# Dealing the pass into the last layer of a four-layer graph network to four engines

## The chip, the cores and the metric

The kernel runs on one core of one Trainium2 chip. The metric is the device time of one execution in microseconds (us); less is better. The profile is one such execution, recorded with every instruction of each engine: PE is TensorE, DVE is VectorE, ACT is ScalarE, POOL is GpSimd, SP is SyncE, and a name with a q (ACTq, SPq) is that engine's sequencer, where DMAs are issued.

## The reference

Four graph layers, each with a layer norm and a relu in front and a residual behind, over 100000 nodes with 64 features and 50000 edges:

```python
edge_index = jnp.stack([src, dst])
h = jnp.maximum(_layernorm(x, axis=-1), 0.0)
x = x + _L0_gnn_ref(h, edge_index, W3, b3, W4, b4)     # two SGConv layers
h = jnp.maximum(_layernorm(x, axis=-1), 0.0)
x = x + _L1_gnn_ref(h, edge_index, edge_attr_64, W, b, eps)
h = jnp.maximum(_layernorm(x, axis=-1), 0.0)
x = x + _L2_gnn_ref(h, attn_w, temp, src, dst)         # K = 8 steps of edge attention
h = jnp.maximum(_layernorm(x, axis=-1), 0.0)
x = x + _L3_gnn_ref(h, src, dst)                       # K = 10 steps
```

The last layer, `_L3_gnn_ref`, takes h = relu(layernorm(x)) as its features `feat`. It starts with `out = w[0] * feat` and adds `w[step + 1] * h` after each of ten steps of gather, scale, sum by destination and scale. So between the third and the fourth layer, every row of x is normed; the normed row is stored for the gathers, and w[0] times that row is added to x.

## The kernel before

Destinations that edges reach are "seats": 128 partitions by 392 columns, one row of 64 f32 each, resident in SBUF as `X`. The columns are worked in NCH = 28 chunks of CH = 14 columns (128 x 896 f32, 448 KB). The pass into the last layer, called pass e here, lies between the end of the attention steps and the first gather of the last layer. It runs over the 28 chunks, and each chunk c uses slot s = c % 2 of two row buffers, `row_be = [rowsB, rowsE]`. `rowsE` is a part of `wide_block`, by which name the profile calls it.

VectorE, for each chunk (`rows_of_e`): `spread_of` makes the variance of each of the 14 rows (14 bn_stats at L1570 and five small operations, L1573 to L1579) and raises `var_ready`. Then `add_rows` of the chunk two before (L2536) adds mix[0] times the made rows to X. Then `scales_of` (L2020, L2025) waits for ScalarE's square root, makes a scale and an offset for each row and raises `scales_ready`.

ScalarE (`seat_pass`): `root(CH)` is the square root (L958) of the next chunk's variance. `scaled_rows` makes the rows of this chunk, one ACTIVATE Relu with scale and bias for each of the 14 columns (L1112). It then waits for the last of them and issues the store of the chunk (L1116) to the table `tab` in HBM. The order is root(c + 1), then rows(c), and before rows(c) it waits on `seats_stored["e"][s]`, the store of the chunk two before.

GpSimd and TensorE have nothing to do in this pass. SyncE issues ten loads of "dead rows" (L547) as soon as the attention steps are over. When the pass is over, VectorE copies the gather indices (L2557), stages the two front rows, and GpSimd scatters the front row (`front_rows`, L575) and starts the gathers of the last layer (L571). X is read and written by the same engine, VectorE, with ScalarE reading it in between.

`Reached` is a register that counts the value awaited. FIRST is 1, a start value of the counting semaphores. `fresh()` clears VectorE's own step semaphore, by which it orders its dependent instructions (`nth()`).

`seat_pass` serves pass a too, the same pass into the first layer, with `row_ac` as its buffers. The functions that the change touches:

Of the kernel before, what the change touches and what calls it, by code (L numbers as in the profile page):

```python
# [3 lines left out]
def _build(nc, x, src, dst, edge_attr, W3, b3, W4, b4, W1, b1, eps, attn_w, temp, out):  # L4
# [7 lines left out]
    ALU = mybir.AluOpType  # L12
# [5 lines left out]
    N, E, D = _N, _E, _D  # L18
    HID = W3.shape[0]
    CH = 14  # L20
    NCH = 28
# [26 lines left out]
    with ctx:  # L48
# [3 lines left out]
        def sem(name):  # L52
            return ctx.enter_context(nc.semaphore(name))
# [21 lines left out]
        X = sb("X", [P, XC, D])  # L75
# [59 lines left out]
        mixb = sb("mixb", [P, K3 + 1])  # L135
        wk = sb("wk", [P, 1])
        scales = sb("scales", [P, 2, 2, CH])
# [3 lines left out]
        G = sb("G", [P, 2, CH, AW])  # L141
# [14 lines left out]
        xm = sb("xm", [P, CH, D])  # L156
        st = sb("st", [P, CH, 6])
        lnw = sb("lnw", [P, 6, CH])
# [107 lines left out]
        widest_loaded = sem("widest_loaded")  # L266
        order_ready = sem("order_ready")
        x_gathered = [sem("x_gathered0"), sem("x_gathered1")]
        x_front = sem("x_front")
        gathered = [sem("gathered0"), sem("gathered1")]  # L270
        gathered3 = [sem("gathered3_0"), sem("gathered3_1")]
# [70 lines left out]
        FIRST = 1  # L342
# [11 lines left out]
        def seat_rows(k, c):  # L354

            return seats(tab, SEAT0 + KINDS.index(k) % 2 * EP, c)
# [10 lines left out]
        def wide(t, n=D):  # L367

            return t.unsqueeze(2).to_broadcast([t.shape[0], t.shape[1], n])
# [25 lines left out]
        def staged_rows(k, c):  # L395

            at = KINDS.index(k) * D
            return staged[:, ds(c * CH, CH), at:at + D]
# [7 lines left out]
        def _(sp):  # L406
# [138 lines left out]
            sp.wait_ge(step_done, K2 + 1)  # L545
            for n in range(K3):
                sp.dma_start(dead_rows[n], staged_rows("e", n)).then_inc(dead_gathered, 16)  # L547
            for n in range(K3):
                sp.wait_ge(dead_ready, n + 1)
                sp.dma_start(seats(alt_e, 0, SPLIT + (n - 1) % K3), dead_rows[(n - 1) % K3]).then_inc(dead_stored, 16)  # L550

        @block.gpsimd
        def _(pool):
# [324 lines left out]
            def attention_end(to):  # L878

                front_sums(to, F_SEAT, F_TSEAT, AW)  # L880
                front_rows(to, F_SEAT_W, FR[:, 0, :], False)
                pool.wait_ge(step_done, r_sd.more(1))
                pool.sem_inc(pool_waited, 1)
# [6 lines left out]
                    attention_end(to)  # L890
            narrow_sweep(alt_d, K2, AW, gathered, gathered_rest)
            attention_end(even_d)
            for s in (0, 1):
                pool.wait_ge(seats_stored["e"][s], FIRST + 16 * NCH // 2)
            pool.sem_inc(pool_waited, 1)
            front_rows(tab, F_TAB_W, rowsE[:, 0, :])
# [51 lines left out]
        def _(act):  # L948
# [153 lines left out]
            def seat_pass(k, rows):  # L1102

                r_to = [Reached(act, f"act_pass_{k}{s}", FIRST) for s in (0, 1)]

                def scaled_rows(c, s):
                    act.wait_ge(seats_stored[k][s], r_to[s].reg)
                    r_to[s].skip(16)
                    act.wait_ge(scales_ready, r_scales.more(1))
                    part = X[:, ds(c * CH, CH), :]  # L1110
                    for j in range(CH):
                        last = nc.scalar.activation(rows[s][:, j, :], part[:, j, :], ACT.Relu,  # L1112
                                                    bias=scales[:, s, 1, j:j + 1], scale=scales[:, s, 0, j:j + 1])
                    last.then_inc(scaled, 1)
                    act.wait_ge(scaled, r_scaled.more(1))
                    act.dma_start(seat_rows(k, c), rows[s][:, :, :]).then_inc(seats_stored[k][s], 16)  # L1116

                root(CH)
                with act.Fori(0, NCH // 2 - 1) as i:
                    for s in (0, 1):  # L1120
                        root(CH)
                        scaled_rows(2 * i + s, s)
                root(CH)
                scaled_rows(NCH - 2, 0)
                scaled_rows(NCH - 1, 1)
                root(2)
# [260 lines left out]
        def _(dve):  # L1387
# [22 lines left out]
            def nth():  # L1410

                steps[0] += 1
                return steps[0]

            def fresh():

                dve.sem_clear(dve_step)
                steps[0] = 0
# [175 lines left out]
            def xcols(c):  # L1594
                return X[:, ds(c * CH, CH), :]
# [933 lines left out]
            with dve.Fori(2, K2 + 1) as k:  # L2529
                fresh()  # L2530
                step_d(k)
            def add_rows(c, s):

                dve.wait_ge(scaled, r_scaled.more(1))
                part = xcols(c)
                v.scalar_tensor_tensor(part, row_be[s][:, :, :], mixb[:, 0:1], part, ALU.mult, ALU.add).then_inc(dve_step, 1)  # L2536
                dve.wait_ge(dve_step, nth())

            def rows_of_e(c, s, before=None):

                spread_of(xcols(c), CH)
                if before is not None:
                    add_rows(before, s)
                scales_of(c, s)

            fresh()
            for s in (0, 1):
                rows_of_e(s, s)
            with dve.Fori(1, NCH // 2) as i:
                fresh()  # L2550
                for s in (0, 1):
                    rows_of_e(2 * i + s, s, 2 * i + (s - 2))
            for s in (0, 1):
                add_rows(NCH - 2 + s, s)
            for s in (0, 1):
                dve.wait_ge(seats_stored["e"][s], FIRST + 16 * NCH // 2)
            v.tensor_copy(idxC[:, :], idxA[:, :]).then_inc(dve_step, 1)  # L2557
# [167 lines left out]
```

## Time and profile before

| what | value |
|---|---|
| median of 3 runs | 8325.15 us (8324.16 to 8325.87) |
| the profiled execution, its time | 8323.41 us |
| its span in the trace | 8321.7 us |
| DVE busy | 5424.0 us (65%) |
| POOL busy | 5607.8 us (67%) |
| ACT busy | 822.4 us (10%) |
| PE busy | 1660.0 us (20%) |

Busy times are of the whole span of the program, whose stages have different limits; pass e is one short stage of it. The chain that ended last is the profile's own path from the last instruction back to the first: at each step to what released it, or to the instruction before it on its engine.

### The profile page before, as it was taken

What the parts mean: (1) busy time and instruction counts of PE and PEld (TensorE: products, weight loads), DVE (VectorE), ACT (ScalarE), POOL (GpSimd) and SP (SyncE); (2) the same over time, 40 slices, a digit from 0 to 9 for tenths busy, and PEclk for the clock granted to TensorE, in tenths of its full rate; (3) what the DMA queues carried; (4) which work ended last, traced back from release to release, by engine and by line L of the source; (5) the groups of instructions that cost most, each with busy time, mean ns of one, the idle gap of its engine ahead of it and who ended that gap; (6) DMA issues with size and microseconds to landing.
All of it is one profiled execution on the core that took longest, in us unless ns stands there. A gap on an engine that the chain in (4) does not pass through costs nothing.

```text
span 8321.7 us, 61168 instructions
## 1 busy us (share of the span) xinstructions
PE 1660.0 (20%) x7784; PEld 1203.9 (14%) x7784; DVE 5424.0 (65%) x18625; ACT 822.4 (10%) x2010; POOL 5607.8 (67%) x5356
## 2 busy tenths in 40 slices
PE   5744444211354035500022102000000000000000
PEld 1233333211243023400022101000000000000000
DVE  6778787768988633367788788666556664445520
ACT  0011111100121521100000000000006000000000
POOL 6777767647777767577677572666640767777777
PEclk8755555555555555555555555555555555555555
DMA  7033434210355334834444213143322222433310
GB/s 262 1 89 94 96 87 98 63 34 21 95 123 128 102 91 121 272 89 111 122 110 109 63 49 83 45 44 46 41 33 88 49 60 49 42 44 43 38 22 19
DMA packets 1198008, 661.32 MB, mean 79 GB/s; under 512 B 1057323, under 2 KB 1070560, under 8 KB 1195204
## 3 DMA queue, kind: packets, MB, share of 16 engines
q10 hardware_dynamic: 880608, 373.78, 16.3%
q0 software_dynamic: 174720, 155.54, 12.9%
q1 hardware_dynamic: 142436, 129.95, 5.3%
q14 instruction: 238, 1.95, 0.1%
q8 instruction: 6, 0.10, 0.0%
HBM read 236.69 MB, written 425.58 MB: 80 GB/s over the span
## 4 chain that ended last, share of the span: by engine, by line
DVE 37%; POOL 30%; issue 19%; DMA 6%; ACT 3%; PE 2%; DVEq 1%; ACTq 1%; POOLq 0%; SPq 0%
POOL G L571 18%; POOL X L571 7%; DVE G L2106 6%; DVE st L1570 4%; POOL out L575 4%; ACT wide_block L1112 2%; DVE xm L1587 2%; DVE X L1545 2%; DVE wide_block L1591 2%; PE TR L1271 1%; DVE X L1544 1%; POOL wide_block L571 1%; DVE G L2418 1%; DVE agg L1668 1%; DVE xm L1600 1%
## 5 line engine op out<-in xcount | busy, mean ns | idle before, releaser
L571 POOL DMA_INDIRECT G<-tab,idxA x1008 | 1079.4, 1071 | 344.5 <-issue 323.6
L571 POOL DMA_INDIRECT X<-flagtab,X x588 | 624.5, 1062 | 231.1 <-issue 230.2
L571 POOL DMA_INDIRECT G<-alt_e,idxC x420 | 435.8, 1038 | 145.9 <-issue 133.4
L575 POOL DMA_INDIRECT seatmap<-X x392 | 406.4, 1037 | 165.2 <-issue 129.0
L571 POOL DMA_INDIRECT X<-lookup,X x392 | 424.5, 1083 | 132.9 <-issue 126.3
L571 POOL DMA_INDIRECT X<-in_x,dst_gat x392 | 423.7, 1081 | 124.9 <-issue 124.9
L1261 PE MATMUL TR<-w4T,shared 128*128 128x64 f32 x2356 | 468.8, 390 | 156.5 <-ACT shared L976 156.5
L571 POOL DMA_INDIRECT G<-alt_d,idxC x392 | 399.3, 1019 | 142.2 <-issue 135.5
L1570 DVE BATCH_NORM_STATS2 st<-xin 128x6 f32<-128x64 f32 x3136 | 419.3, 211 | 114.6 <-issue 62.2
L1261 PEld LDWEIGHTS TR<-w4T,shared 128*128 128x128 f32 x2356 | 455.4, 300 | 250.1 <-issue 250.1
L1278 PE MATMUL HP<-ident,tcar 128*64 128x128 f32 (+1 forms) x21 | 8.7, 415 | 2263.2 <-DVEq L1495 2252.6
L1238 PE MATMUL TR<-ident,wide_block 128*128 128x128 f32 x882 | 219.0, 425 | 773.8 <-DVEq L1637 534.1
L958 ACT ACTIVATE lnw<-lnw,lneps 128x14 f32<-128x14 f32 (+1 forms) x340 | 104.3, 307 | 2633.6 <-DVEq L1581 2581.0
L2585 DVE TENSOR_TENSOR G<-G,chn 128x320 f32<-128x320 f32 (+2 forms) x165 | 82.7, 534 | 407.7 <-DMA G<-alt_e,idxC 202.6
L571 POOL DMA_INDIRECT shared<-in_edge_attr,eidx x252 | 284.2, 1128 | 79.4 <-issue 79.1
L2106 DVE SCALAR_TENSOR_TENSOR G<-G,chn 128x64 f32<-128x64 f32 x1092 | 312.1, 286 | 39.1
L1278 PEld LDWEIGHTS HP<-ident,tcar 128*64 128x64 f32 (+1 forms) x21 | 3.2, 150 | 2266.5 <-issue 2266.5
L1271 PE MATMUL TR<-w1Te,hT 64*128 64x64 f32 x1568 | 182.0, 420 | 731.3 <-ACT hT L966 731.3
L571 POOL DMA_INDIRECT G<-even_e,idxC x252 | 261.6, 1038 | 83.4 <-issue 74.0
L571 POOL DMA_INDIRECT G<-tab,idxC x252 | 260.0, 1032 | 79.7 <-issue 79.7
L575 POOL DMA_INDIRECT out<-X,dst_out x252 | 244.9, 972 | 97.5 <-issue 81.8
L966 ACT ACTIVATE hT<-TR 128x512 f32<-128x512 f32 (+1 forms) x358 | 183.9, 537 | 1209.6 <-PE TR L1238 1190.3
(517 smaller groups left out, 7671.0 us busy)
## 6 DMA issues: line engine op xcount, KB each, us to landing
tab<-wide_block ACTq DMA_DIRECT2D x294, 448.0 KB, 3.8
tab<-rowsB ACTq DMA_DIRECT2D x98, 448.0 KB, 2.7
xin<-tab SPq DMA_DIRECT2D x84, 448.0 KB
raw<-G ACTq DMA_DIRECT2D x84, 448.0 KB
xin<-in_x SPq DMA_DIRECT2D x56, 448.0 KB
tab<-wide_block ACTq DMA_DIRECT2D x2, 12544.0 KB, 56.3
out<-shared ACTq DMA_DIRECT2D x56, 448.0 KB, 5.8
staged<-wide_block SPq DMA_DIRECT2D x20, 1120.0 KB, 5.9
```

The source lines that it names most:

```text
L571: pool.indirect_dma_start(to, None, table, bass.IndirectOffsetOnAxis(ap=index, axis=0), bounds_check=bound, oob_is_err=False).then_inc(s, 16)
L575: pool.indirect_dma_start(table, bass.IndirectOffsetOnAxis(ap=index, axis=0), frm, None, bounds_check=bound, oob_is_err=False).then_inc(s, 16)
L966: last = nc.scalar.activation(hT[:, a:b, :].rearrange("p a b -> p (a b)"), T[:, a * P:b * P], ACT.Copy)
L1112: last = nc.scalar.activation(rows[s][:, j, :], part[:, j, :], ACT.Relu, bias=scales[:, s, 1, j:j + 1], scale=scales[:, s, 0, j:j + 1])
L1238: last = nc.tensor.transpose(T[:, q * P:(q + 1) * P], rows[:, 2 * q:2 * q + 2, :].rearrange("p a b -> p (a b)"), ident[:, :])
L1261: last = nc.tensor.matmul(T[:, r * D:(r + 1) * D], U[:, r % 2, r // 2, :], w4T[:, :], start=True, stop=True)
L1271: last = nc.tensor.matmul(T[:, at:at + D], hT[h * D:(h + 1) * D, r // 2, :], w[h * D:(h + 1) * D, :], start=True, stop=True)
L1545: v.tensor_scalar(hot_lo[:, j % NHOT, :], iota16[:, :], chn[:, 1, j:j + 1], None, ALU.is_equal).then_inc(dve_step, 1)
L1570: last = v.bn_stats(st[:, r, :], xr[:, r, :])
L1587: v.scalar_tensor_tensor(xm[:, a0:a1, :], wide(m_sum[:, a0:a1]), -0.5, xr[:, a0:a1, :], ALU.mult, ALU.add)
L1591: v.scalar_tensor_tensor(to, xm[:, 0:R, :], 0.0, wide(rs), ALU.max, ALU.mult).then_inc(dve_step, 1)
L2106: v.scalar_tensor_tensor(G[:, s, j, 0:W], before, go[:, j:j + 1], G[:, s, j, 0:W], ALU.mult, ALU.add).then_inc(dve_step, 1)
```

## The change

In pass e, the work on a chunk is dealt out anew. Pass a stays as it was.

- ScalarE makes the first 11 (`SHARE = CH - 3`) of the 14 rows and no longer waits for its own last row to issue the store. It also waits on `added[s]`, the addition of the chunk two before, since X and the row buffers are shared with GpSimd.
- VectorE makes the other three rows by two operations on 128 x 192 (subtract the mean into `xm`, then relu and scale into `row_be`), after `scales_of` of the chunk. Ahead of the second it waits for the store and the addition of the chunk two before. Its loop over pairs is written out as 28 chunks, and `add_rows` is gone from it.
- GpSimd, idle until now, waits for both parts of the chunk, multiplies all 14 rows by mix[0] into `G`, and adds `G` to X.
- SyncE waits for both parts of the chunk and issues the store. In its queue this stands behind the ten loads of the dead rows.

```diff
@@ semaphores
+        added = [sem("added0"), sem("added1")]
+        last_rows = sem("last_rows")
+        SHARE = CH - 3
@@ SyncE, behind the ten loads of dead rows
+            for c in range(NCH):
+                sp.wait_ge(scaled, NCH + c + 1)
+                sp.wait_ge(last_rows, c + 1)
+                sp.dma_start(seat_rows("e", c), row_be[c % 2][:, :, :]).then_inc(seats_stored["e"][c % 2], 16)
@@ GpSimd, behind attention_end
+            for c in range(NCH):
+                s = c % 2
+                part = X[:, c * CH:c * CH + CH, :]
+                pool.wait_ge(scaled, NCH + c + 1)
+                pool.wait_ge(last_rows, c + 1)
+                pool.tensor_scalar(G[:, s, :, 0:D], row_be[s][:, :, :], mixb[:, 0:1], None, ALU.mult).then_inc(pool_step, 1)
+                pool.wait_ge(pool_step, r_step.more(1))
+                pool.sem_inc(pool_waited, 1)
+                pool.tensor_tensor(part, part, G[:, s, :, 0:D], ALU.add).then_inc(added[s], 1)
             for s in (0, 1):
+                pool.wait_ge(added[s], FIRST + NCH // 2)
                 pool.wait_ge(seats_stored["e"][s], FIRST + 16 * NCH // 2)
@@ ScalarE, scaled_rows
                     act.wait_ge(scales_ready, r_scales.more(1))
+                    if k == "e":
+                        act.wait_ge(added[s], r_added[s].reg)
+                        r_added[s].skip(1)
                     part = X[:, ds(c * CH, CH), :]
-                    for j in range(CH):
+                    for j in range(CH if k == "a" else SHARE):
...
                     last.then_inc(scaled, 1)
-                    act.wait_ge(scaled, r_scaled.more(1))
-                    act.dma_start(seat_rows(k, c), rows[s][:, :, :]).then_inc(seats_stored[k][s], 16)
+                    if k == "a":
+                        act.wait_ge(scaled, r_scaled.more(1))
+                        act.dma_start(seat_rows(k, c), rows[s][:, :, :]).then_inc(seats_stored[k][s], 16)
@@ VectorE
-            def add_rows(c, s):
-
-                dve.wait_ge(scaled, r_scaled.more(1))
-                part = xcols(c)
-                v.scalar_tensor_tensor(part, row_be[s][:, :, :], mixb[:, 0:1], part, ALU.mult, ALU.add).then_inc(dve_step, 1)
-                dve.wait_ge(dve_step, nth())
-
-            def rows_of_e(c, s, before=None):
+            def rows_of_e(c, s):
 
                 spread_of(xcols(c), CH)
-                if before is not None:
-                    add_rows(before, s)
                 scales_of(c, s)
-
-            fresh()
+                part = X[:, c * CH + SHARE:c * CH + CH, :]
+                v.scalar_tensor_tensor(xm[:, SHARE:CH, :], wide(lnw[:, 0, SHARE:CH]), -0.5, part,
+                                       ALU.mult, ALU.add).then_inc(dve_step, 1)
+                dve.wait_ge(dve_step, nth())
+                if c >= 2:
+                    dve.wait_ge(seats_stored["e"][s], FIRST + 16 * (c // 2))
+                    dve.wait_ge(added[s], FIRST + c // 2)
+                v.scalar_tensor_tensor(row_be[s][:, SHARE:CH, :], xm[:, SHARE:CH, :], 0.0,
+                                       wide(scales[:, s, 0, SHARE:CH]), ALU.max, ALU.mult).then_inc(dve_step, 1)
+                dve.wait_ge(dve_step, nth())
+                dve.sem_inc(last_rows, 1)
+
             for s in (0, 1):
-                rows_of_e(s, s)
-            with dve.Fori(1, NCH // 2) as i:
-                fresh()
-                for s in (0, 1):
-                    rows_of_e(2 * i + s, s, 2 * i + (s - 2))
+                dve.sem_inc(added[s], FIRST)
+            for c in range(NCH):
+                if c % 2 == 0:
+                    fresh()
+                rows_of_e(c, c % 2)
             for s in (0, 1):
-                add_rows(NCH - 2 + s, s)
+                dve.wait_ge(added[s], FIRST + NCH // 2)
```

## Rows read from the trace of the kernel before

**Rows 1.** Timeline of ScalarE, start of pass e: start us, us, engine, line, operation.

```profile
6267.14 0.31 ACT L958 ACTIVATE lnw<-lnw,lneps 128x14 f32<-128x14 f32 x1 [11.19 <-DVEq L1581]
6270.85 0.31 ACT L958 ACTIVATE lnw<-lnw,lneps 128x14 f32<-128x14 f32 x1 [3.41 <-DVEq L1581]
6271.07 4.74 ACT L1112 ACTIVATE rowsB<-X,scales 128x64 f32 x14
6275.98 0.34 ACTq L1116 DMA_DIRECT2D tab<-rowsB  x1
6276.43 0.31 ACT L958 ACTIVATE lnw<-lnw,lneps 128x14 f32<-128x14 f32 x1 [0.62 <-ACT rowsB L1112]
6276.67 4.74 ACT L1112 ACTIVATE wide_block<-X,scales 128x64 f32 x14
6281.57 0.34 ACTq L1116 DMA_DIRECT2D tab<-wide_block  x1
6282.25 0.31 ACT L958 ACTIVATE lnw<-lnw,lneps 128x14 f32<-128x14 f32 x1 [0.84 <-ACT wide_block L1112]
```

**Rows 2.** Busy time of each engine in the stretch of pass e.

```profile
6264.35:6431.71 167.36, 0.00 (x0) 0.00 (x0) 116.49 (x617) 139.28 (x420) 0.00 (x0) 0.50 0.32 98
```

**Rows 3.** Timeline of VectorE, the first two chunks of pass e.

```profile
6264.35 1.87 DVE L1570 BATCH_NORM_STATS2 st<-X 128x6 f32<-128x64 f32 x14 [0.37 <-DVE eidx L2331]
6266.26 0.18 DVE L1573 TENSOR_TENSOR lnw<-st 128x14 f32<-128x14 f32 x1
...
6266.87 0.17 DVE L1579 SCALAR_TENSOR_TENSOR lnw<-lnw 128x14 f32<-128x14 f32 x1
6267.47 0.24 DVE L2020 RECIPROCAL scales<-lnw 128x14 f32<-128x14 f32 x1 [0.43 <-ACT lnw L958]
6267.75 0.17 DVE L2025 SCALAR_TENSOR_TENSOR scales<-lnw,scales 128x14 f32<-128x14 f32 x1
6268.07 1.87 DVE L1570 BATCH_NORM_STATS2 st<-X 128x6 f32<-128x64 f32 x14
...
6276.00 1.15 DVE L2536 SCALAR_TENSOR_TENSOR X<-rowsB,mixb,X 128x896 f32 x1 [1.16 <-ACT rowsB L1112]
```

**Rows 4.** Timeline of all engines, end of pass e.

```profile
6424.32 4.74 ACT L1112 ACTIVATE wide_block<-X,scales 128x64 f32<-128x64 f32 x14 [0.50 <-ACT rowsB L1112]
6429.10 0.35 ACTq L1116 DMA_DIRECT2D tab<-wide_block  x1
6431.71 0.36 DVE L2557 COPY idxC<-idxA 128x392 int32<-128x392 int32 x1 [1.46 <-DMA tab<-wide_block]
```

**Rows 5.** Groups of VectorE by line and shape: busy us, mean ns of one.

```profile
L1587 DVE SCALAR_TENSOR_TENSOR xm<-lnw,X 128x320 f32<-128x320 f32 x112 | 50.1, 489 | 8.8 <-DVE lnw L1579 8.8
L1587 DVE SCALAR_TENSOR_TENSOR xm<-lnw,X 128x256 f32<-128x256 f32 x56 | 23.7, 423 | 0.0
```

**Rows 6.** Groups of GpSimd by line and shape, computing operations.

```profile
L615 POOL COPY X<-X 125x800 f32<-125x800 f32 x1 | 1.0, 1034 | 6.0 <-DMA X<-seatmap 6.0
L587 POOL IOTA X<- 128x800 f16 x1 | 0.8, 802 | 0.2 <-POOL X L584 0.2
L591 POOL MEMSET ident<- 128x128 f32 x1 | 0.2, 204 | 0.2 <-POOL X L587 0.2
```

**Rows 7.** Timelines of GpSimd and of VectorE around GpSimd's copy.

```profile
585.16 1.03 POOL L615 COPY X<-X 125x800 f32<-125x800 f32 x1 [5.98 <-DMA X<-seatmap]
...
584.32 1.09 DVE L1591 SCALAR_TENSOR_TENSOR wide_block<-xm,lnw 128x896 f32<-128x896 f32 x1
```

**Rows 8.** Timeline of all engines, in the last layer.

```profile
6460.99 4.25 DVE L2096 SCALAR_TENSOR_TENSOR G<-G,chn 128x64 f32<-128x64 f32 x13
6461.07 1.00 POOL L571 DMA_INDIRECT G<-tab,idxC  x1 [0.30 <-issue]
6462.37 1.01 POOL L571 DMA_INDIRECT G<-tab,idxC  x1 [0.30 <-issue]
```

**Rows 9.** DMA issues of pass e's stretch: count, size, us to landing.

```profile
tab<-rowsB ACTq DMA_DIRECT2D x14, 448.0 KB, 2.5
xin<-staged SPq DMA_DIRECT2D x2, 448.0 KB, 7.3
```

**Rows 10.** Timeline of SyncE's queue, its last issues in pass e.

```profile
6273.48 4.16 SPq L547 DMA_DIRECT2D wide_block<-staged  x2
```

More of the change, by code:

```diff
@@ L1104, in seat_pass @@
                 r_to = [Reached(act, f"act_pass_{k}{s}", FIRST) for s in (0, 1)]
+                r_added = [Reached(act, f"act_added_{k}{s}", FIRST) for s in (0, 1)]
                 def scaled_rows(c, s):
@@ L2531, in _ @@
                 step_d(k)
-            def add_rows(c, s):
-                dve.wait_ge(scaled, r_scaled.more(1))
-                part = xcols(c)
-                v.scalar_tensor_tensor(part, row_be[s][:, :, :], mixb[:, 0:1], part, ALU.mult, ALU.add).then_inc(dve_step, 1)
-                dve.wait_ge(dve_step, nth())
-            def rows_of_e(c, s, before=None):
-                spread_of(xcols(c), CH)
-                if before is not None:
-                    add_rows(before, s)
-                scales_of(c, s)
-            fresh()
-            for s in (0, 1):
-                rows_of_e(s, s)
-            with dve.Fori(1, NCH // 2) as i:
-                fresh()
-                for s in (0, 1):
-                    rows_of_e(2 * i + s, s, 2 * i + (s - 2))
+            def rows_of_e(c, s):
+                spread_of(xcols(c), CH)
+                scales_of(c, s)
+                part = X[:, c * CH + SHARE:c * CH + CH, :]
+                v.scalar_tensor_tensor(xm[:, SHARE:CH, :], wide(lnw[:, 0, SHARE:CH]), -0.5, part,
+                                       ALU.mult, ALU.add).then_inc(dve_step, 1)
+                dve.wait_ge(dve_step, nth())
+                if c >= 2:
[5 more added lines that the diff above has]
+                dve.sem_inc(last_rows, 1)
+            for s in (0, 1):
+                dve.sem_inc(added[s], FIRST)
[3 more added lines that the diff above has]
+                rows_of_e(c, c % 2)
             for s in (0, 1):
-                add_rows(NCH - 2 + s, s)
+                dve.wait_ge(added[s], FIRST + NCH // 2)
             for s in (0, 1):
```

## The prediction

> **What bounds the kernel now.** I read the page first. VectorE and GpSimd are busy for about two thirds of the span and ScalarE for a tenth, but these are averages over stages. The change touches one stage only, the pass into the last layer, so I went to the windows view for that stretch. From the first bn_stats at 6264.35 to the copy of the indices at 6431.71 it takes 167.4 us, 2.0% of the span. ScalarE is busy for 139.3 us of it, VectorE for 116.5, GpSimd for nothing [rows 2]. Then the timeline of ScalarE: 14 rows take 4.74 us. Around them stand the wait for the last row, the issue of the store (0.34), the root and the loop's branch. From the root at 6270.85 to the root at 6282.25 two chunks lie, 11.4 us, so 5.70 a chunk, in which the engine only waits for itself [rows 1]. VectorE is not late: its addition starts when the rows are there [rows 3]. So ScalarE bounds the pass. Outside of the chunks there is a start (the first rows begin at 6271.07, 6.72 us in) and an end: the last row is made at 6429.06, and the pass ends 2.65 us later, when the last store has landed [rows 1, 4].
>
> **ScalarE's part.** Fourteen rows take 4.74, the last of them about 0.42 whole, so one every 0.332 us and eleven take 3.74. The root costs 0.22 (6270.85 to 6271.07) [rows 1]. The wait for the last row and the issue (0.6 to 0.8 us of idle time ahead of the root) go, and one wait that is as a rule satisfied comes. ScalarE alone would need some 4.1 to 4.3 us a chunk. This would be a gain of 1.5 us a chunk, 40 us in all, if nothing else became late.
>
> **VectorE's part.** The addition (1.15 us) goes. The spread takes 6264.35 to 6267.04, 2.69; the root's round trip 0.43; reciprocal and offset up to the next bn_stats 0.60 [rows 3]. Two new operations of 192 elements come. The same form takes 0.489 us at 320 and 0.423 at 256, so 0.36 at 192 [rows 5]; with the 0.15 us that each of its dependent steps waits (6267.92 to 6268.07 [rows 3]) both are 1.02. Sum 4.74 us a chunk. That the loop is written out takes its branch away, which lay in VectorE's spare time: nothing.
>
> **GpSimd's part.** The trace of before shows it multiplying or adding nowhere. The nearest rows are a copy of 800 elements, 1.03 us, and an iota of 800, which only writes, 0.80 [rows 6]. For the product (one input, 896 elements) this gives 0.90 by the iota and 1.16 by the copy; I take 1.0. The sum has two inputs. At least the second input costs what the first adds to the iota, 1.03 + 0.23 = 1.26 at 800 or 1.41 at 896; at most it costs a second copy, 2.3. I take the middle, 1.85. Between the two stands 0.17, as between its steps at the start (0.2 idle [rows 6]). Together P = 3.0 us, from 2.5 to 3.6. The Trainium skill (GPSIMD Engine Reference, section 3.1) measured 4497 ns for an add of 2048 f32. Scaled to 896 this is an estimate of 1.97 us; with it the sum below would come out 3 us later. No run here shows it yet.
>
> **SyncE's part.** The store's issue leaves ScalarE. It is queued behind ten loads of dead rows, whose issue ends at 6277.6 [rows 10] and which take 7 us to land [rows 9]. The first chunk is ready at about 6275.8, so the first store is some us late, once: 0 to 3 us. Later stores land 2.5 us after their issue [rows 9], 2.8 with the wait ahead, a little less than P, so they are hidden behind GpSimd.
>
> **The wait that comes.** VectorE writes its three rows into the slot of the chunk two before. So it waits for that chunk's addition, and behind it in its queue stand the spread of the next chunk, with it ScalarE's next root, and with it ScalarE's rows. The ring over two chunks is: addition seen 0.2, three rows 0.36 + 0.15, spread 2.69, root 0.10 + 0.22, eleven rows 3.74, seen by GpSimd 0.2, then P. That is 7.66 + P = 10.7, or 5.33 a chunk, if each engine ran at its own pace. The great saving on ScalarE shrinks to 0.37 a chunk before any collision.
>
> **The collision.** The copy of GpSimd began at 585.16, while VectorE's operation with two SBUF inputs ran until 585.41. It took 1.03, which is 0.23 more than the iota of the same length, and 0.25 us of it lay beside that operation [rows 6, 7]. It can be read as a copy that waited for VectorE to let go of SBUF. Against it speaks that GpSimd's indirect DMAs take their usual 1.00 us right beside thirteen such operations, and these their usual time too [rows 8]; but an indirect DMA is no stream over the tile. The Trainium skill (SBUF — State Buffer, "Who interferes with whom") says that a VectorE instruction with two SBUF inputs and a GpSimd instruction that reads SBUF exclude each other for a whole instruction, and that it is the later one that blocks. By that rule the sum is the one below; without it, the ring's. The copy's row agrees, weakly.
>
> What it costs here if they exclude each other: eight of VectorE's operations of a chunk have two SBUF inputs, all but bn_stats and the reciprocal. After a spread, ScalarE's rows end 0.32 + 3.74 later, and GpSimd starts at 4.26. VectorE starts the next bn_stats 0.43 + 0.60 + 1.02 = 2.05 after the same point, ends them at 3.93 and is between 3.96 and 4.74 in its five small operations, just when GpSimd comes. They need SBUF by turns: VectorE stands for the product, slips one small operation in, and stands for the sum. A chunk is then 4.74 + 1.0 + 1.85 = 7.59 us.
>
> **The sum.** Start: 6.72, the 1.02 of chunk 0's own three rows, eleven rows 3.74: 11.5. Then 26 chunks by 7.59: 197.3. The last chunk has no spread behind it: 3.9. The end: 0.2, P, 0.2: 3.4. Together 216.1, against 167.4: 48.7 us more. The profiled execution took 8323.41 and the median of the runs is 8325.15; on the median this is 8374. By the other reading it is 11.5 + 26 by 5.33 + 3.9 + 3.4 = 157.4, 10 us less. The two are even at 5.72 us a chunk, and 0.2% (16.7 us, about what a measurement of this kernel can tell from no change) slower begins at 6.36.
>
> **The rivals.**
> 1. They exclude each other (the forecast): 7.59 a chunk, 8374. With P's parts from 2.31 to 3.46 it is 7.05 to 8.20, so 8359 to 8390. Chance 0.55.
> 2. They exclude each other for one of the two operations only, because the small ones of VectorE are through before the product begins, or because the product doesn't hold them: 4.74 + 1.0 to 4.74 + 1.85, thus 5.7 to 6.6 a chunk, 8326 to 8348. Chance 0.08.
> 3. No exclusion, the ring bounds: 5.33 a chunk, 8315; with P from 2.5 to 3.6 and up to 3 us for the late first store 8309 to 8327. For it speak the indirect DMAs of rows 8. Chance 0.27.
> 4. GpSimd is much dearer than its copy, with no exclusion. The ring passes 5.72 a chunk when P is over 3.8, and 6.36 when P is over 5.1; at P = 6, 6.8 a chunk, 8357. Nothing but the lack of a row speaks for it. Chance 0.06.
> 5. The other side: the buffers don't bind and VectorE's own 4.74 a chunk does: 11.5 + 123.2 + 7.3 = 142, 25 us less, 8300. For that P would have to be under 1.8 and the store to land within 1.6 us, and neither row allows it [rows 6, 9]. Chance 0.04.
>
> The range that holds the time 8 times in 10 goes from 8312, in the middle of rival 3, to 8394, a bit above rival 1's end. The likeliest case's own is 8359 to 8390. Faster by over 0.2%: rival 5 and the edge of rival 3, 0.06. Slower by over 0.2%: rival 1, the upper halves of rivals 2 and 4, 0.63. Within: 0.31.
>
> **What the changed profile would show.** ScalarE: groups of eleven rows in 3.74 us, no store. GpSimd: 28 products and 28 sums; their starts, one from the next, give P. VectorE: if there is exclusion, one of L1573 to L1579 stands for an us or more beside GpSimd's product or sum, in its own duration or as a gap ahead of it, in nearly every chunk, and chunks come every 7 to 8 us. If not, the small operations keep their 0.1 us steps beside GpSimd, and the only long wait of VectorE is ahead of its second new operation, on the addition of two chunks before, with chunks every 5.3 us. What follows the pass shouldn't change. The forecast is wrong if GpSimd's reads go on beside VectorE's, or if they take turns by element and not by instruction.

## The result and the profile after

Over 14 runs each, the changed kernel takes 8338.13 us (8334.27 to 8346.81) and the kernel before 8324.65 us (8316.77 to 8331.14). The ratio is 1.0018 with an interval of 1.0011 to 1.0025: a little slower, just inside the 0.2% that I took as no change. The forecast was 8374, 49 us more; 13.5 us more came. The measured time lies in the range, but the range reached from the middle of rival 3 to beyond rival 1 and so says little; the forecast move is over three times too large.

The profiled execution took 8338.17 us. Its pass e runs from the first bn_stats at 6262.47 to the copy of the indices at 6447.8, so 185.3 us against 167.4 [rows 2], 17.9 us more. The whole execution is 14.8 us longer; the other 3 us lie outside the pass, less than the executions scatter there.

First, the windows view of that stretch. Its columns are, here and in [rows 2], the length in us, the busy us (and number of instructions) of PE, PE's weight loads, DVE, ACT and POOL, the clock granted to TensorE, the share of the DMA engines, and GB/s:

```profile
6262.47:6447.80 185.33, 0.00 (x0) 0.00 (x0) 141.97 (x645) 112.50 (x336) 124.78 (x56) 0.50 0.29 89
```

ScalarE's work fell from 139.3 to 112.5 us. VectorE's rose from 116.5 to 142.0, though its additions of 1.15 us each are gone. GpSimd has 124.8. No engine is busy for the whole stretch, so a chain over engines sets the pace. The groups of GpSimd in the pass:

```profile
L908 POOL TENSOR_TENSOR X<-X,G 128x896 f32<-128x896 f32 x28 | 54.0, 1928 | 5.1 <-POOL G L905 5.1
L905 POOL TENSOR_SCALAR G<-wide_block,mixb 128x896 f32<-128x896 f32 x14 | 35.4, 2530 | 18.9 <-ACT wide_block L1133 18.9
```

And the two groups of VectorE, in the stretch 6264 to 6430, that take much longer than their work:

```profile
L2559 DVE SCALAR_TENSOR_TENSOR xm<-lnw,X 128x192 f32<-128x192 f32 x27 | 26.6, 985 | 4.0
L2047 DVE SCALAR_TENSOR_TENSOR scales<-lnw,scales 128x14 f32<-128x14 f32 x27 | 22.4, 831 | 0.9
```

The sum takes 1.93 us, as I had it (1.85). The product takes 2.53 us, and I had 1.0. VectorE's offset, 0.17 us when alone, takes 0.83 on average, and the mean's subtraction 0.99 in place of 0.36. The reason shows in the timeline of the first meeting, GpSimd's product of chunk 0 beside VectorE's spread of chunk 2:

```profile
6274.10 2.53 POOL L905 TENSOR_SCALAR G<-rowsB,mixb 128x896 f32<-128x896 f32 x1 [17.48 <-ACT rowsB L1133]
6274.18 0.95 DVE L1599 TENSOR_TENSOR lnw<-lnw 128x14 f32<-128x14 f32 x1
6275.16 0.17 DVE L1601 SCALAR_TENSOR_TENSOR lnw<-lnw 128x14 f32<-128x14 f32 x1
...
6276.82 1.95 POOL L908 TENSOR_TENSOR X<-X,G 128x896 f32<-128x896 f32 x1 [0.19 <-POOL G L905]
```

L1599 starts inside the product and takes 0.95 us in place of 0.17. It ends 1.03 us after the product's start, while the product goes on for 1.5 us more, beside the next operation, which keeps its 0.17. So the product keeps VectorE out for about its first microsecond only. From the middle of the pass, where the pace has settled:

```profile
6341.54 1.94 POOL L908 TENSOR_TENSOR X<-X,G 128x896 f32<-128x896 f32 x1 [0.18 <-POOL G L905]
6341.67 1.84 DVE L2047 SCALAR_TENSOR_TENSOR scales<-lnw,scales 128x14 f32<-128x14 f32 x1
6343.66 0.36 DVE L2559 SCALAR_TENSOR_TENSOR xm<-lnw,X 128x192 f32<-128x192 f32 x1
6344.06 0.36 DVE L2565 SCALAR_TENSOR_TENSOR rowsB<-xm,scales 128x192 f32<-128x192 f32 x1
6344.57 1.87 DVE L1592 BATCH_NORM_STATS2 st<-X 128x6 f32<-128x64 f32 x14 [0.15 <-DVE rowsB L2565]
...
6345.18 2.53 POOL L905 TENSOR_SCALAR G<-wide_block,mixb 128x896 f32<-128x896 f32 x1 [1.70 <-ACT wide_block L1133]
6346.47 0.18 DVE L1595 TENSOR_TENSOR lnw<-st 128x14 f32<-128x14 f32 x1
...
6347.09 0.17 DVE L1601 SCALAR_TENSOR_TENSOR lnw<-lnw 128x14 f32<-128x14 f32 x1
6347.35 0.31 ACT L975 ACTIVATE lnw<-lnw,lneps 128x14 f32<-128x14 f32 x1 [2.27 <-DVEq L1603]
6347.62 3.75 ACT L1133 ACTIVATE rowsB<-X,scales 128x64 f32 x11
...
6351.47 2.53 POOL L905 TENSOR_SCALAR G<-rowsB,mixb 128x896 f32<-128x896 f32 x1 [1.68 <-ACT rowsB L1133]
```

Here the ring can be followed. The sum of one even chunk ends at 6343.48. VectorE's offset L2047 began 0.13 us after that sum and ended with it, so the sum keeps it out to its end. But VectorE needs that very sum for its rows two operations later, so nearly all that it stands for would have been a wait anyway. Its rows are done at 6344.42, the next spread at 6347.26, the root starts at 6347.35, ScalarE's rows end at 6351.37 and GpSimd begins at 6351.47. Product, 0.18 and sum end at 6356.12: 12.64 us for two chunks, 6.32 each. Later in the pass the sum meets the operation behind L2047, the mean's subtraction:

```profile
6398.01 1.90 POOL L908 TENSOR_TENSOR X<-X,G 128x896 f32<-128x896 f32 x1 [0.18 <-POOL G L905]
6398.26 1.87 DVE L2559 SCALAR_TENSOR_TENSOR xm<-lnw,X 128x192 f32<-128x192 f32 x1
```

There less work is left behind the sum, and the products come every 6.18 us. Over chunks 2 to 26 they start 6.23 us apart on average.

### The profile page after: what moved, and what is told of

It is laid out like the page before. It is cut to its first block and busy times, and to the rows that moved or that the text cites. A ratio compares the mean times of both kernels' runs of the same rounds, so it can differ in the third digit from the quotient of the medians.

```text
span 8336.5 us, 60751 instructions
## 1 busy us (share of the span) xinstructions
PE 1684.4 (20%) x7784; PEld 1223.0 (15%) x7784; DVE 5448.3 (65%) x18653; ACT 795.5 (10%) x1926; POOL 5731.8 (69%) x5412
## 5 line engine op out<-in xcount | busy, mean ns | idle before, releaser
L1609 DVE SCALAR_TENSOR_TENSOR xm<-lnw,xin 128x320 f32<-128x320 f32 (+1 forms) x672 | 279.1, 470 | 34.0 <-DVE lnw L1601 25.8
```

The source lines that it names most:

```text
L1609: v.scalar_tensor_tensor(xm[:, a0:a1, :], wide(m_sum[:, a0:a1]), -0.5, xr[:, a0:a1, :], ALU.mult, ALU.add)
```

## The experiments

All compare pass e, from the first bn_stats to the copy of the indices, in the profiled execution; the time of the whole kernel scatters by some us even where nothing is changed, so of kernels with one run only the pass is judged. "Ring" is the reading that the chain over two chunks sets the pace; "exclusion" is that of my forecast, that VectorE's work plus the time it stands shut out of SBUF sets it. P is GpSimd's part of a chunk, product, gap and sum, 4.64 us in the changed kernel.

| kernel | pass, us | a chunk, us | median time, us | ratio to before |
|---|---|---|---|---|
| before | 167.4 | 5.70 | 8324.65 | |
| changed | 185.3 | 6.18 to 6.32 | 8338.13 | 1.0018 [1.0011, 1.0025] |
| 1, no multiply and add | 151.8 | 5.0 | 8312.22 (one run) | |
| 2, product contiguous | 188.5 | | 8346.17 (one run) | |
| 3, immediate scalar | 185.6 | | 8334.80 (one run) | |
| 4, next spread first | 178.1 | 6.07 | 8344.37 | 1.0013 [1.0004, 1.0022] |
| 5, SyncE's stores alone | 158.1 | 5.31 | 8322.75 | 0.9987 [0.9978, 0.9996] |
| 6, 14 rows on ScalarE | 168.7 | 5.64 | 8330.10 | 0.9996 [0.9987, 1.0005] |
| 7, product as tensor_tensor | 205.6 | 7.15 | 8380.21 (one run) | |
| 8, one input from PSUM | 186.7 | 6.30 | 8344.78 (one run) | |
| 9, seven and eight | 174.6 | 5.85 | 8340.47 (one run) | |
| 10, four and eight | 149.9 | 4.88 | 8310.76 | 0.9974 [0.9965, 0.9984] |
| 11, five, written out | 148.5 | 4.87 | 8311.79 | 0.9975 [0.9965, 0.9985] |

The pace of a chunk is half the distance of every other root or product in the middle of the pass. The kernel before, measured again beside the experiments, had 8329.60 us (one run) beside 1 to 3, 8333.62 beside 4 to 7 and 8331.35 beside 8 to 11. The changed kernel's ratio is to 8324.65, the others' are to these, so times of different groups are not compared with each other.

**1. GpSimd waits and signals, but computes nothing.** The addition to X is left out.

```diff
-                pool.tensor_scalar(G[:, s, :, 0:D], row_be[s][:, :, :], mixb[:, 0:1], None, ALU.mult).then_inc(pool_step, 1)
-                pool.wait_ge(pool_step, r_step.more(1))
-                pool.sem_inc(pool_waited, 1)
-                pool.tensor_tensor(part, part, G[:, s, :, 0:D], ALU.add).then_inc(added[s], 1)
+                pool.sem_inc(added[s], 1)
```

> GpSimd waits and signals as in the changed kernel, but multiplies and adds nothing: the addition of mix[0] times the rows to X is left out. In the changed kernel the pass takes 185.4 us, 6.3 a chunk. Ring theory (the ring over two chunks sets the pace, and VectorE's standing beside GpSimd costs at most 0.4 us a chunk): the ring is now closed by the store, which lands 2.8 us after the rows, so (0.1 + 0.36 + 0.15 + 2.69 + 0.10 + 0.27 + 3.75 + 2.8) / 2 = 5.1 us a chunk and a pass of about 151 us. Exclusion theory (VectorE's chunk plus what it stands for SBUF): nothing to stand for, so VectorE's own 4.74 a chunk, a pass of about 142 us. Both: L1599, L2047 and L2559 of VectorE are back at 0.17, 0.17 and 0.36 us in every chunk.

The pass took 151.8 us, as the ring has it, and the stretched operations are back at their own lengths. VectorE's busy time in the pass is 104.1 us where the changed kernel has 142.0, with 644 and 645 instructions. So in the changed kernel VectorE stands shut out for 37.8 us in all, 1.35 a chunk.

```profile
6265.87:6417.72 151.85, 0.00 (x0) 0.00 (x0) 104.14 (x644) 112.47 (x336) 0.00 (x0) 0.50 0.35 109
```

VectorE now waits a little for the store, ahead of its rows:

```profile
6348.72 0.36 DVE L2556 SCALAR_TENSOR_TENSOR xm<-lnw,X 128x192 f32<-128x192 f32 x1
6349.58 0.36 DVE L2562 SCALAR_TENSOR_TENSOR wide_block<-xm,scales 128x192 f32<-128x192 f32 x1 [0.51 <-DMA tab<-wide_block]
```

So GpSimd's two operations are worth 33.5 us of the pass, and the slot's ring is closed by the next thing, the store, when they are gone.

**2 and 3. Why the product is dear.** Two suspects: the pitch of its output (the rows of G lie 67 elements apart, with 64 in use), and its scalar, which it reads from SBUF by a pointer. In experiment 2 the sum reads the product from the contiguous buffers too (not shown):

```diff
-                pool.tensor_scalar(G[:, s, :, 0:D], row_be[s][:, :, :], mixb[:, 0:1], None, ALU.mult).then_inc(pool_step, 1)
+                pool.tensor_scalar([rowsA, hT as 14 x 64][s], row_be[s][:, :, :], mixb[:, 0:1], None, ALU.mult).then_inc(pool_step, 1)
+++ in the other kernel
+                pool.tensor_scalar(G[:, s, :, 0:D], row_be[s][:, :, :], mix[0], None, ALU.mult).then_inc(pool_step, 1)
```

> GpSimd's product goes to contiguous buffers of 14 x 64 that are idle in this pass, instead of G, whose rows have a pitch of 67 elements. If the pitch makes the product dear (2.53 us), it falls to about 1.2 (its copy of 800 elements took 1.03), P falls from 4.64 to 3.3, and by the ring a chunk takes 6.3 - 0.67 = 5.65 us, the pass about 167. If the pitch has nothing to do with it, product and pass stay at 2.53 and 185 us. By the exclusion theory VectorE's chunk plus the sum, 4.74 + 1.93 = 6.7, stays whatever the product costs.

> GpSimd's product takes mix[0] as an immediate and not from a column of SBUF. If the pointer to the scalar makes the product dear (2.53 us), it falls to about 1.2, and the pass to about 167 us by the ring (5.65 a chunk). If it is the pitch of the output or the multiplication itself, product and pass stay at 2.53 and 185 us.

The groups of GpSimd, first of the contiguous one, then of the one with the immediate:

```profile
L905 POOL TENSOR_SCALAR wide_block<-rowsB,mixb 128x896 f32<-128x896 f32 x13 | 32.8, 2522 | 39.8 <-ACT rowsB L1133 39.8
```

```profile
L905 POOL TENSOR_SCALAR G<-rowsB 128x896 f32<-128x896 f32 x14 | 34.4, 2456 | 43.7 <-ACT rowsB L1133 43.7
```

Neither is it: 2.52 and 2.46 us. The passes, 188.5 and 185.6 us, get no shorter than the changed kernel's, so both suspects are out. In experiment 2 the sum took 2.07 us in place of 1.93; by the ring this is some 2 of its 3 us more.

**4. The next spread ahead of the wait.** This takes the spread, ScalarE's root and its rows out from behind the wait for the addition.

```diff
-                spread_of(xcols(c), CH)
                 scales_of(c, s)
...
                 dve.wait_ge(dve_step, nth())
+                if c + 1 < NCH:
+                    spread_of(xcols(c + 1), CH)
                 if c >= 2:
                     dve.wait_ge(seats_stored["e"][s], FIRST + 16 * (c // 2))
                     dve.wait_ge(added[s], FIRST + c // 2)
```

> The changed kernel with one thing moved: VectorE makes the spread of the next chunk ahead of its wait for the store and the addition of two chunks before, and its three rows behind it. This cuts the ring: ScalarE's next root no longer stands behind GpSimd. Ring theory, if the ring alone set the pace: the pace is then the slowest engine's, GpSimd with 2.53 + 0.18 + 1.93 + 0.1 = 4.75 or VectorE with 4.74 us a chunk, so a pass of about 145 us and a time 20 us under before. Exclusion theory: GpSimd is then busy nearly without a break, so VectorE stands for each product (about 1 us, as L1599 in the changed kernel) and each sum (1.9), 4.74 + 2.9 = 7.6 a chunk, a pass of about 220 us and a time some 50 us over before.

The pass took 178.1 us, 7 less than the changed kernel's and far from either theory's number. The ring is cut, but VectorE stands on L2047 for 1.27 us on average (1448 ns against 174), beside the sum:

```profile
L2047 DVE SCALAR_TENSOR_TENSOR scales<-lnw,scales 128x14 f32<-128x14 f32 x28 | 40.6, 1448 | 1.0
```

VectorE's 4.74 and this 1.27 are 6.01, and the pace is 6.07. So without the ring the exclusion bounds, at less than half the price that I had put on it, since the product mostly finds VectorE in its bn_stats. The time of the whole kernel does not tell it from the changed one: the ratios to before, 1.0013 and 1.0018, have intervals that overlap.

**5. SyncE's stores alone.** The kernel before; ScalarE's wait and store go for pass e, SyncE waits on `scaled` and issues them.

```diff
+            for c in range(NCH):
+                sp.wait_ge(scaled, NCH + c + 1)
+                sp.dma_start(seat_rows("e", c), row_be[c % 2][:, :, :]).then_inc(seats_stored["e"][c % 2], 16)
...
-                    act.wait_ge(scaled, r_scaled.more(1))
-                    act.dma_start(seat_rows(k, c), rows[s][:, :, :]).then_inc(seats_stored[k][s], 16)
+                    if k == "a":
+                        act.wait_ge(scaled, r_scaled.more(1))
+                        act.dma_start(seat_rows(k, c), rows[s][:, :, :]).then_inc(seats_stored[k][s], 16)
```

> The kernel before with one part of the change alone: SyncE issues the stores of the pass, all 14 rows stay with ScalarE and the addition with VectorE. ScalarE needs 0.27 + 4.74 + 0.1 = 5.1 us a chunk in place of 5.70, VectorE 2.69 + 0.43 + 0.60 + 1.27 = 5.0. GpSimd has no part in it, so both theories expect 5.1 to 5.2 a chunk, a pass of 150 to 153 us, 14 to 17 us less than before: about 8310, ratio 0.998.

158.1 us: 9.3 less than before, not the 14 to 17 expected. Every other chunk took 5.05, the others 5.56. The reason is in the timeline of VectorE: 0.78 us of idle time ahead of each second bn_stats, where its loop branches back, and 0.27 ahead of the others. The kernel before had the same gap, but there VectorE waited 0.6 to 0.9 us for ScalarE's rows in every chunk anyway. Experiment 11 tests this.

```profile
6343.08 0.17 DVE L2029 SCALAR_TENSOR_TENSOR scales<-lnw,scales 128x14 f32<-128x14 f32 x1
6344.03 1.88 DVE L1574 BATCH_NORM_STATS2 st<-X 128x6 f32 x14 [0.78 <-DVE scales L2029]
```

**6. All 14 rows on ScalarE, the addition on GpSimd.** `SHARE = CH`, and VectorE's two operations and its waits on the slot go; SyncE stores.

```diff
-        SHARE = CH - 3
+        SHARE = CH
...
```

> The changed kernel without VectorE's share: ScalarE makes all 14 rows, SyncE stores, GpSimd multiplies and adds. VectorE has 3.72 us of work a chunk and waits for no addition, so the ring over the spread is gone. Ring theory: ScalarE's 5.1 a chunk is the pace (GpSimd 4.75; ScalarE's own wait for the addition (4.74 + 0.1 + 4.64 + 0.15) / 2 = 4.8), a pass of about 154 us, 13 less than before. Exclusion theory: VectorE's 3.72 plus what it stands, up to 2.9, is 6.6 a chunk, a pass of about 190 us, 23 more than before.

168.7 us, between the two. By the starts of the products, every other chunk took 4.84 us, as fast as ScalarE can, the others 6.44. In those VectorE stands for the sum with the first and for the product with the fourth of its small operations, and ScalarE's root waits for both:

```profile
6339.89 1.95 POOL L908 TENSOR_TENSOR X<-X,G 128x896 f32<-128x896 f32 x1 [0.18 <-POOL G L905]
6340.35 1.52 DVE L1595 TENSOR_TENSOR lnw<-st 128x14 f32<-128x14 f32 x1
...
6342.01 2.53 POOL L905 TENSOR_SCALAR G<-wide_block,mixb 128x896 f32<-128x896 f32 x1 [0.17 <-ACT wide_block L1133]
6342.10 0.94 DVE L1599 TENSOR_TENSOR lnw<-lnw 128x14 f32<-128x14 f32 x1
```

This kernel has no ring over the spread, and yet its pass is 20 us longer than that of experiment 11, which also has 14 rows on ScalarE, stores on SyncE and a written-out loop. That the exclusion is what takes this back is read from these rows; it was not tried here with an input in PSUM.

**7. The product as a tensor_tensor.** The scalar is broadcast over the tile as a second input.

```diff
-                pool.tensor_scalar(G[:, s, :, 0:D], row_be[s][:, :, :], mixb[:, 0:1], None, ALU.mult).then_inc(pool_step, 1)
+                pool.tensor_tensor(G[:, s, :, 0:D], row_be[s][:, :, :], mixb[:, 0:1].unsqueeze(2).to_broadcast([P, CH, D]),
+                                   ALU.mult).then_inc(pool_step, 1)
```

> GpSimd's product as a tensor_tensor with mix[0] broadcast over the tile, in place of the tensor_scalar that took 2.53 us. If it is that kind of instruction that is dear, it takes 1.9 to 2.1 us as the sum does, P falls by 0.5, by the ring a chunk takes 6.05 and the pass about 178 us. If the multiplication is dear on GpSimd, it stays at 2.5 or more and so does the pass.

The product took 1.68 us, a third less, and the pass took 205.6, 20 us more. The ring expected 178. This is the run that taught most. Its timeline:

```profile
6346.47 1.68 POOL L905 TENSOR_TENSOR G<-rowsB,mixb 128x896 f32<-128x896 f32 x1 [4.43 <-ACT rowsB L1133]
6346.60 1.57 DVE L1599 TENSOR_TENSOR lnw<-lnw 128x14 f32<-128x14 f32 x1
6348.21 0.17 DVE L1601 SCALAR_TENSOR_TENSOR lnw<-lnw 128x14 f32<-128x14 f32 x1
6348.32 1.95 POOL L908 TENSOR_TENSOR X<-X,G 128x896 f32<-128x896 f32 x1 [0.18 <-POOL G L905]
```

This product keeps VectorE out to its end, and what it keeps out is L1599, a link ahead of the root. In every other chunk both of GpSimd's operations meet VectorE there, the product at L1595 and the sum at L1599:

```profile
6340.14 1.89 POOL L908 TENSOR_TENSOR X<-X,G 128x896 f32<-128x896 f32 x1 [0.18 <-POOL G L905]
6340.22 1.84 DVE L1599 TENSOR_TENSOR lnw<-lnw 128x14 f32<-128x14 f32 x1
...
6352.57 1.68 POOL L905 TENSOR_TENSOR G<-wide_block,mixb 128x896 f32<-128x896 f32 x1 [2.30 <-ACT wide_block L1133]
6353.25 1.04 DVE L1595 TENSOR_TENSOR lnw<-st 128x14 f32<-128x14 f32 x1
```

Such a delay falls on the path, where one on L2047 beside the sum is hidden by the wait for that sum. Here VectorE stands for 62.4 us in all (166.5 us busy against 104.1 in experiment 1), 2.2 a chunk. My way of adding, with these lengths, would give 4.74 + 1.68 + 1.93 = 8.35 a chunk, so even here it is too dear; 7.15 came.

**8 and 9. No VectorE operation with two inputs in SBUF.** PSUM is the other memory on the chip in which this kernel keeps tiles (`HP`, `TR`). VectorE copies the statistics to it and takes one input of each small operation from there; the mean and the subtracted rows lie in PSUM too. Once on the changed kernel, once on that of experiment 7.

```diff
-                v.tensor_tensor(m_sum, st[:, 0:R, 1], st[:, 0:R, 4], ALU.add)
-                v.tensor_tensor(m2, st[:, 0:R, 2], st[:, 0:R, 5], ALU.add)
-                v.tensor_tensor(m_dif, st[:, 0:R, 1], st[:, 0:R, 4], ALU.subtract).then_inc(dve_step, 1)
-                dve.wait_ge(dve_step, nth())
-                v.tensor_tensor(m_dif, m_dif, m_dif, ALU.mult).then_inc(dve_step, 1)
+                v.tensor_copy(st_e, st[:, :, :]).then_inc(dve_step, 1)
+                dve.wait_ge(dve_step, nth())
+                v.tensor_tensor(m_sum, st[:, :, 1], st_e[:, :, 4], ALU.add)
+                v.tensor_tensor(m2, st[:, :, 2], st_e[:, :, 5], ALU.add)
+                v.tensor_tensor(dif_p, st[:, :, 1], st_e[:, :, 4], ALU.subtract)
+                v.tensor_tensor(dif, st[:, :, 1], st_e[:, :, 4], ALU.subtract).then_inc(dve_step, 1)
+                dve.wait_ge(dve_step, nth())
+                v.tensor_tensor(sq, dif, dif_p, ALU.mult).then_inc(dve_step, 1)
...
```

> The changed kernel with one input of each of VectorE's small operations in PSUM, so that none of its operations in the pass has two SBUF inputs while GpSimd computes. It costs VectorE a copy of the statistics and one more subtraction, about 0.4 us a chunk. Exclusion by two SBUF inputs: no operation of VectorE is stretched any more, neither beside the product nor beside the sum; the scales and the mean's subtraction are done when the sum ends, which saves 0.2 us a chunk. The ring is then (0.2 + 0.51 + 3.1 + 0.1 + 0.27 + 3.75 + 0.1 + 2.53 + 0.18 + 1.93) / 2 = 6.33 a chunk, so the pass stays at about 185 us. If exclusion has nothing to do with SBUF inputs, the stretched operations stay and a chunk takes 6.7.

> As the run before, with GpSimd's product as a tensor_tensor (1.68 us). With both inputs of VectorE's operations in SBUF that kernel took 7.15 us a chunk and 205.6 us for the pass. If exclusion made it so, the ring sets the pace now: 6.33 less half of 0.85, 5.9 a chunk, a pass of about 173 us, in spite of 0.4 us more work on VectorE. If the tensor_tensor was slow for another reason, a chunk stays at 7.1 to 7.5 and the pass over 200 us.

On the changed kernel the pass stayed, 186.7 us at 6.30 a chunk, as the ring has it. On that of experiment 7 it fell from 205.6 to 174.6 us, 5.85 a chunk (173 and 5.9 expected), though VectorE does more. Beside the product and the sum, every operation keeps its length:

```profile
6344.19 1.68 POOL L908 TENSOR_TENSOR G<-rowsB,mixb 128x896 f32<-128x896 f32 x1 [2.76 <-ACT rowsB L1136]
6344.35 0.18 DVE L2566 TENSOR_TENSOR HP<-st,HP 128x14 f32<-128x14 f32 x1
...
6344.81 0.18 DVE L2571 TENSOR_TENSOR HP<-lnw,HP 128x14 f32<-128x14 f32 x1
6345.03 0.17 DVE L2573 SCALAR_TENSOR_TENSOR lnw<-HP,lnw 128x14 f32<-128x14 f32 x1
...
6346.05 1.95 POOL L911 TENSOR_TENSOR X<-X,G 128x896 f32<-128x896 f32 x1 [0.18 <-POOL G L908]
6346.37 0.37 DVE L2582 SCALAR_TENSOR_TENSOR TR<-HP,X 128x192 f32<-128x192 f32 x1
```

Experiments 7 and 9 have the same GpSimd instructions and differ in where VectorE's inputs lie. That shows the exclusion and its condition: two inputs in SBUF on VectorE's side. The Trainium skill (SBUF — State Buffer, "Who interferes with whom") has this condition, and the runs agree. It also has the lock held for the whole instruction. The sum and the tensor_tensor product agree with that, the tensor_scalar product doesn't: it let VectorE in after 1.03 of its 2.53 us.

**10. Both hindrances gone.** The edits of experiments 4 and 8 together.

> The changed kernel with both hindrances gone: VectorE makes the next spread ahead of its wait for the addition (which alone gave 6.07 a chunk and a pass of 178.1), and one input of its operations lies in PSUM. Ring and exclusion together explain the changed kernel if the pace is now the slowest engine's: VectorE 4.74 + 0.4 = 5.15, GpSimd 4.75 a chunk, a pass of about 155 us, 12 less than before: about 8318 beside 8330, ratio 0.9985. If a third thing holds it, a chunk stays near 6.

149.9 us, 4.88 a chunk, which is what GpSimd (4.64 and a gap of 0.18 between chunks) and VectorE need by themselves. It is 5 us less than expected: in this order VectorE's rows are made while it waits for the root, so that part of the round trip is no longer idle. The time is 0.9974 of before [0.9965, 0.9984]. So ring and exclusion together explain why the changed kernel is slower than its engines' own work; no third thing is needed.

**11. SyncE's stores, VectorE's loop written out.** Experiment 5 with a `for` in place of the `Fori` over pairs.

```diff
-            with dve.Fori(1, NCH // 2) as i:
+            for i in range(1, NCH // 2):
```

> The kernel before with SyncE's stores (5.31 us a chunk in pairs of 5.05 and 5.56, pass 158.1) and with VectorE's loop over pairs written out. The longer chunk of each pair holds 0.5 us of VectorE's loop branch ahead of bn_stats; without it both chunks take 5.05 to 5.1, the pass about 152 us, 15 less than before: ratio about 0.998.

148.5 us, 4.87 a chunk, 0.9975 of before [0.9965, 0.9985]. It is 3.5 us less than expected, since the chunks without the branch became faster too, 4.87 for 5.05. In experiment 5 the variance of such a chunk was ready at 6341.16, just when ScalarE's rows ended, and the root started 0.1 us later; here it is ready before that, and the root starts 0.1 us ahead of the rows' end. The kernel is as fast as that of experiment 10, with no work on GpSimd and none of the rows on VectorE.

## Why the prediction was wrong, step by step

**What bounds the kernel before: right.** With the store off ScalarE, and with nothing else, a chunk falls to 4.87 us once VectorE's branch is out of the way (experiments 5 and 11).

**ScalarE's and VectorE's parts: right.** Eleven rows take 3.75 us (3.74), the two operations 0.36 each (0.36). I put the branch of VectorE's loop at nothing, as it lay in VectorE's spare time. No run has the change with the loop kept. Where VectorE is near the bound the branch costs 9.6 us of pass (158.1 and 148.5 us, experiments 5 and 11).

**GpSimd's part: the first step that failed.** I took 1.0 us for the product, by a copy and an iota, with 1.16 as the upper end. It measured 2.53, outside my bounds. The bound was no bound: the price of a copy (1.03 us for 800 elements) does not carry over to this engine's tensor_scalar. The sum was right (1.93 for 1.85; the estimate from the Trainium skill, GPSIMD Engine Reference, section 3.1, was 1.97). P was 4.64 and not 3.0.

**SyncE's part: nearly right.** The first store was issued at 6275.76, and VectorE's rows of chunk 2 waited for it until 6281.57, 2.8 us after the sum that they needed had ended (6278.77). I had 0 to 3, and put none of it into the sum.

```profile
6275.76 2.21 SPq L554 DMA_DIRECT2D tab<-rowsB  x1
6281.57 0.36 DVE L2565 SCALAR_TENSOR_TENSOR rowsB<-xm,scales 128x192 f32<-128x192 f32 x1 [4.85 <-DMA tab<-rowsB]
```

**The ring: right in form.** 7.66 + P with the measured P is 12.3 for two chunks, 6.15 each; measured 6.18 to 6.32. Experiment 1 gave the expected 151 us where the store closes it.

**The collision: the exclusion is there, but it is not added to VectorE's chunk. This is the step that made the forecast too large.** GpSimd's operations and VectorE's with two SBUF inputs do exclude each other (experiments 7 to 9). But "VectorE stands for the product, slips one small operation in, and stands for the sum" holds neither for this product nor at this place. The product lets VectorE in after about 1 us. It is so long that the sum begins when VectorE has passed its small operations and the root, and stands at L2047 or L2559; there the wait for that same sum would have come anyway. And at the settled pace the product begins 1.3 us before the first small operation (6345.18 and 6346.47), and has let go by then. I had expected one of the five small operations to stand beside GpSimd in nearly every chunk; their means are 0.17 to 0.23 us.

I added 2.85 us to each chunk for the collision. VectorE did stand for 1.35 a chunk, but at most 0.2 of it reached the pace: 6.32 a chunk in the middle and 6.23 on average, where the ring alone gives 6.15. Experiment 8 agrees: with no exclusion and 0.4 us more work in the ring, 0.2 a chunk, it has 6.30. The term was 7.59 in my sum and measured 6.23. The wrong price of the product does not explain that: with the measured lengths my own way of adding gives 4.74 + 2.53 + 1.93 = 9.20 a chunk, further off. Where the product is shorter and keeps VectorE out to its end, a larger part of the standing counts, 7.15 a chunk for 8.35 by my way (experiment 7).

**The direction: luck.** I forecast a slower kernel because of the collision. It was slower because the product was dear and the ring carries P. With P = 3.0, as I had it, the ring alone gives 5.33 a chunk and a faster kernel. What the collision would cost beside a product that short, no run shows; experiment 7 says that it need not be small.

**The sum, with measured terms.** To the first product 11.6, two chunks with the late store 14.9, 24 by 6.225 = 149.4, the last chunk 4.6, the end 4.7: 185.2 us, 17.9 more than before.

**The rivals.** Rival 4 came nearest, GpSimd dearer than its copy with the ring as the bound: P = 4.64 lies between its points of 3.8 and 5.1. It was stated with no exclusion, though, and there is one; it just costs little here. By its ring with the measured P the pass is 11.5 + 26 by 6.15 + 3.9 + 5.0 = 180.3 us. Of the 5 us more that came, 2.8 are the late first store and some 2 the collision. I gave it 0.06, since nothing but the lack of a row spoke for it. That lack was the reason to give it more.

## What to carry to other kernels

Work handed to an idle engine lengthens every ring of buffers that it stands in. Write down the ring with all its members, divide by the number of buffers, and see first what is queued behind its wait: here the wait stood ahead of the next chunk's first step, and moving it behind that step took 7 us off the pass (experiment 4) and no more work.

When GpSimd computes, look at which VectorE operations beside it have two inputs in SBUF, and whether they stand ahead of a wait that hides the delay or on the path. One input in PSUM took the collision away here (experiments 8 to 10). A shorter GpSimd instruction can make the kernel slower: the one of experiment 7 also shut VectorE out to its end, and moved the collision onto the path.

Try a part of a change by itself. Here one part, the stores on SyncE, was worth 0.25% with a loop written out; the other two parts used it up.

## What the runs showed that I had not expected

- GpSimd's tensor_scalar multiply on 128 x 896 f32 takes 2.53 us with a pointer and 2.46 with an immediate, whatever the pitch of the output. As a tensor_tensor with the scalar broadcast it takes 1.68, and an add of two full tiles 1.93 (2.07 in experiment 2, with the second input contiguous). Its copy of 800 elements took 1.03.
- The tensor_scalar let VectorE's operation with two SBUF inputs in 1.03 us after its start, of 2.53; the tensor_tensor forms held it to their end. Why the one lets go early is open.
- The stretch of a shut-out operation shows in its own duration and not as idle time ahead of it. So VectorE's busy time in the pass rose to 142.0 us in the changed kernel and to 166.5 in experiment 7, with the same number of instructions (645).
- Where the pass starts scatters between kernels that are the same up to there, from 6257.7 (experiment 3) to 6277.0 us (experiment 7). About 13 of the 57 us by which experiment 7's execution is longer than the one of before lie ahead of the pass. What follows the pass scatters too, from 1887.7 us (experiment 8) to 1895.9 (experiment 7). The cause of either is open.
